# Four small re-orderings in a four-layer graph network: split pairs of layer 2 from its second chunk on, one exponential ahead of a row sum, row tiles ahead of their sets, one piece read a beat sooner

## The reference

```python
# layer 1: attention with 4 heads over all nodes, masked by adj
scores = einsum(q, k) * SCALE + graph_bias * adj
attn   = softmax(where(adj == 0, -1e9, scores));  out = (attn @ v) @ Wout + bout
# layer 2: graph attention
Wh = x @ W;  e = leaky_relu((Wh @ a[:256])[:, None] + (Wh @ a[256:])[None, :], 0.2)
h  = softmax(where((adj > 0) | eye, e, -9e15), axis=1) @ Wh
# layers 3 and 4: graph convolution with degrees
d = adj.sum(axis=1) ** -0.5
layer 3: (d[:, None] * adj * d[None, :]) @ x @ W.T + b
layer 4: relu((d[:, None] * adj * d[None, :]) @ x @ W)
```

## Time and profile before

| | before |
|---|---|
| median of 3 runs | 2970.06 us (2968.12 to 2972.88) |
| the profiled execution | 2971.03 us, span 2969.0 us |
| PE busy | 2917.2 us, 98% |
| DVE busy | 2134.3 us, 72% |
| ACT busy | 1901.1 us, 64% |
| POOL busy | 761.4 us, 26% |
| chain that ended last | PE 86%, DVE 6%, DMA 2%, issue 2%, ACT 2%, POOL 1% |
| granted clock of TensorE, mean | 0.996 |

### The profile page before, as it was taken

The page is one execution under the profiler, slowest core; times in us unless marked ns, Lnnn a source line. Parts: engine busy times, 40 slices in busy tenths (PEclk is TensorE's granted clock), DMA queues, the critical chain, the costliest instruction groups (busy, mean ns, idle before and its releaser), DMA issues.

```text
span 2969.0 us, 45931 instructions
## 1 busy us (share of the span) xinstructions
PE 2917.2 (98%) x16828; PEld 2195.2 (74%) x16828; DVE 2134.3 (72%) x3633; ACT 1901.1 (64%) x2755; POOL 761.4 (26%) x458
## 2 busy tenths in 40 slices
PE   8999999999999999999999899999999999999998
PEld 6677777777777777777776565555568888788887
DVE  6777777777777777777766999899745656666564
ACT  4677777777777777777777777777753433533332
POOL 2123321333213331233302455555500101000000
PEclk9999999999999999999999999999999999999999
DMA  6556575565745566456617254554279999989882
GB/s 190 148 158 182 178 210 153 164 185 178 214 140 173 185 186 194 140 180 182 193 57 274 107 185 156 166 174 156 75 179 220 218 206 205 226 214 219 200 205 57
DMA packets 387183, 521.86 MB, mean 176 GB/s; under 512 B 38672, under 2 KB 316432, under 8 KB 370576
## 3 DMA queue, kind: packets, MB, share of 16 engines
q1 hardware_dynamic: 361920, 432.41, 53.0%
q10 hardware_dynamic: 18144, 66.07, 7.1%
q0 software_dynamic: 6896, 20.45, 2.4%
HBM read 430.71 MB, written 88.08 MB: 175 GB/s over the span
## 4 chain that ended last, share of the span: by engine, by line
PE 86%; DVE 6%; DMA 2%; issue 2%; ACT 2%; POOL 1%; SPq 1%; POOLq 0%; DVEq 0%; ACTq 0%
PE at_o L615 15%; PE at_turn L589 11%; PE at_turn L602 10%; PE gl_four L1562 9%; PE gl_quad L1619 7%; PE gl_quad L1620 7%; PE gl_quad L1621 7%; PE at_score L589 5%; PE at_score L602 5%; PE gl_quad L1527 3%; PE at_mixed L624 2%; DVE gl_first_weights L1898 1%; DMA gl_early<-x 1%; DVE gl_first_weights L1851 1%; PE at_mixed L569 1%
## 5 line engine op out<-in xcount | busy, mean ns | idle before, releaser
L726 ACT ACTIVATE at_probs<-at_probs,at_minus_max 128x1024 f32<-128x1024 f32 x512 | 581.6, 1139 | 9.6 <-DVE at_minus_max L880 8.7
L875 DVE CUSTOM_DVE_ANT_0 at_probs<-at_turn,at_bias 128x1024 f32<-128x1024 f32 x336 | 407.9, 1214 | 187.1 <-PE at_turn L589 184.3
L512 POOL TENSOR_SCALAR at_masked<-at_bias 128x512 bf16<-128x512 f32 x180 | 365.4, 2050 | 496.3 <-DMA at_bias<-in_adj 404.2
L735 ACT ACTIVATE at_pT<-at_turn 128x1024 f32<-128x1024 f32 x342 | 346.0, 1024 | 219.7 <-PE at_turn L602 219.7
L615 PE MATMUL at_o<-at_pT,at_values 128*64 128x256 f32 x4096 | 470.3, 382 | 0.0
L1736 ACT ACTIVATE gl_split<-gl_units 128x1024 fp32r<-128x1024 f32 x256 | 262.2, 1057 | 263.5 <-PE gl_quad L1621 263.5
L615 PEld LDWEIGHTS at_o<-at_pT,at_values 128*64 128x64 f32 x4096 | 282.5, 137 | 172.8 <-issue 43.2
L1619 PE MATMUL gl_quad<-gl_split,gl_rows_hi 128*128 128x512 f32 x1024 | 399.7, 390 | 3.8 <-DVE gl_split L1968 3.8
L1620 PE MATMUL gl_quad<-gl_split,gl_rows_hi 128*128 128x512 f32 x1024 | 398.6, 389 | 0.0
L1621 PE MATMUL gl_quad<-gl_split,gl_rows_lo 128*128 128x512 f32 x1024 | 398.4, 389 | 0.0
L589 PE MATMUL at_turn<-at_kT,at_q 128*128 128x512 f32 x1344 | 396.0, 416 | 0.6 <-DVE at_maxima L875 0.6
(11 more groups left out here) (158 smaller groups left out, 4091.1 us busy)
## 6 DMA issues: line engine op xcount, KB each, us to landing
gl_units<-adjT SPq DMA_DIRECT2D x512, 256.0 KB, 8.2
at_bias<-in_adj SPq DMA_DIRECT2D x128, 512.0 KB, 6.1
gl_first_weights<-in_adj SPq DMA_DIRECT2D x32, 2048.0 KB, 9.2
at_values<-v_heads ACTq DMA_DIRECT2D x126, 512.0 KB, 4.1
at_probs<-in_adj SPq DMA_DIRECT2D x208, 256.0 KB, 3.4
adjT<-at_probs SPq DMA_DIRECT2D x832, 64.0 KB, 2.6
gl_early<-x SPq DMA_DIRECT2D x160, 128.0 KB, 2.7
adjT<-gl_early SPq DMA_DIRECT2D x192, 64.0 KB, 1.8
```

Source lines behind the costliest of these rows:

```text
L512: pool.tensor_scalar(masked[:, g % MASKS, :], part, 0.0, MASKED / SCALE, ALU.is_equal, ALU.mult)\
L726: act.activation(part, part, ACT.Exp, bias=minus_max[:, k, t:t + 1], scale=1.0, accum_out=sums[:, k, t, pp:pp + 1]).then_inc(prob_ready, 1)
L735: act.activation(pT[:, j % PT_SLOTS, :], place[:], ACT.Copy).then_inc(pT_ready, 1)
L875: dve.tensor_tensor_reduce(out=ring[:, place_in_ring(u, pp), t, :], in0=place[:], in1=bias[:, t, at], scale=SCALE, scalar=LOWEST, op0=ALU. ...
```

## The change

- `READ_AT`: piece 4 is read by VectorE in beat 14 and no longer in beat 15.
- `LAST_EXP` = 11: in pair 11 of a chunk ScalarE takes the exponential first and the row sum second; in all other pairs the order stays.
- SyncE loads row tiles 13 to 23 ahead of sets 0 and 1, and no longer behind them.
- In the first chunk of layer 2 pairs 10, 12 and 14 are multiplied in float32 like the others. The high and low parts of `wh` are made in the second chunk, the low ones in pairs 3 to 5 (before: 5 to 7 of the first), and behind a new wait for the last product of the first chunk, since they overwrite `wh`. The loads of the third chunk no longer wait for split products of the first.

```diff
-    READ_AT = {7: 0, 9: 1, 11: 2, 13: 3, 15: 4}
+    READ_AT = {7: 0, 9: 1, 11: 2, 13: 3, 14: 4}
...
+    LAST_EXP = PAIRS - QP - 1
...
-                for pair in SPLIT_PAIRS:
+                for pair in SPLIT_PAIRS if c else ():
...
-            for m in range(13):
+            for m in range(24):
                 load_row_tile(1, m)
             load_set(0, 0)
             load_set(0, 1)
-            for m in range(13, 24):
-                load_row_tile(1, m)
             load_set(0, 2)
             load_set(0, 3)
...
-                if pair in SPLIT_PAIRS:
+                if c and pair in SPLIT_PAIRS:
                     i = SPLIT_PAIRS.index(pair)
-                    if c == 0:
+                    if c == 1:
                         pe.wait_ge(wh_lo_ready, i + 1)
-                    pe.wait_ge(pT_lo_ready, len(SPLIT_PAIRS) * c + i + 1)
+                    pe.wait_ge(pT_lo_ready, len(SPLIT_PAIRS) * (c - 1) + i + 1)
...
-                if pair in SPLIT_PAIRS:
+                if c and pair in SPLIT_PAIRS:
                     act.activation(pT_hi[:, g % PT_RING, :], pair_bank[g % 2], ACT.Copy).then_inc(pT_ready, 1)
...
-                    if c == 0 and 2 <= pair < 2 + len(SPLIT_PAIRS):
+                    if c == 1 and 2 <= pair < 2 + len(SPLIT_PAIRS):
                         split_wh_hi(pair - 2)
...
+                    if pair == LAST_EXP:
+                        exponential(ITEMS * c + CT + pair)
                     add_rows(ITEMS * c + LEAD + pair)
-                    if pair < PAIRS - QP:
+                    if pair < LAST_EXP:
                         exponential(ITEMS * c + CT + pair)
...
                 dve.wait_ge(wh_hi_ready, i + 1)
+                dve.wait_ge(multiplied1, PAIRS)
...
-                    if c == 0 and 5 <= pair < 5 + len(SPLIT_PAIRS):
-                        split_wh_lo(pair - 5)
-                    if pair in SPLIT_PAIRS:
+                    if c == 1 and 3 <= pair < 3 + len(SPLIT_PAIRS):
+                        split_wh_lo(pair - 3)
+                    if c and pair in SPLIT_PAIRS:
                         keep_pT_lo(c, pair)
```

## The result

| | before | changed |
|---|---|---|
| median, first session | 2969.09 us (2966.87 to 2972.88, 4 runs) | 2953.11 us (2952.43 to 2954.27, 4 runs) |
| ratio to before | | 0.9944, 95% interval 0.9932 to 0.9955 |
| the profiled execution | 2971.03 us, span 2969.0 | 2952.43 us, span 2950.7 |
| the same comparison in a later session | 2973.58 us (2968.54 to 2977.92, 9 runs) | 2955.98 us (2953.84 to 2956.47, 5 runs) |
| its ratio | | 0.9941, 95% interval 0.9929 to 0.9954 |

What follows compares the result with a forecast made beforehand. TensorE, busy 98% of the span, was taken as the bound. Terms -8.3 + 0.2 - 2.5 - 5.0 - 3.1 = -18.7 us took the profiled 2971.03 to 2952.3, as a median 2951.3 us; range 2945.5 to 2958.

Steps and rivals of the forecast that it cites:

- Part 1, first chunk: Layer 2's first chunk: pairs 10, 12, 14 plain, the 13.86 us step becomes 4.31; -8.3 us, ends -10 and -5.
- 0.5 off at turn 4: ScalarE's copy in pair 3 that holds turn 4 moves from first to second chunk: 0.5 us off, 0.5 on.
- Part 1, what is late next: VectorE's shift for the second chunk comes at 1704.1, ScalarE wants it at about 1706: 2 us early.
- Part 1, second chunk: VectorE's 1.8 us of `wh` differences move into pairs 3 to 5, making pair 10's low part 1.2 us later.
- I take 0.2 ... ends 0 and 1.5: Second chunk: TensorE's stall for pair 10's late low part, zero to 0.5 us, taken as +0.2.
- Part 2: Exponential ahead of the row sum in pair 11: -3.9 us over chunks two to seven, +1.4 new stall, net -2.5.
- The degrees' delay: Seventh chunk's later row sum delays the degrees and ScalarE's copy of pair 1 in the last chunk: +1.4 us.
- Part 3: Last chunk: row tiles 13 to 23 issued before the sets remove waits of ScalarE and TensorE; -5.0 us, ends -5.0 and -2.
- a sign of being wrong: ScalarE waiting for row tile 24 in the last chunk, listed among what would show the forecast wrong.
- the fourth rival: Tile 24 late behind four sets and the store, TensorE waits in pairs 12 to 14; price 5, 2956.3 us; chance 0.11.
- the sixth: Rival, slower than before: tile 24 lands so late (2208) that the sum turns positive; price 22, 2973 us; chance 0.03.
- Part 4: Layer 1's end of projections: piece 4 read in beat 14 removes TensorE's 3.18 us wait; -3.1 us, ends -3.5 and -1.

Runs made afterwards that it cites:

- Part 1 undone: Changed kernel with layer 2's first-chunk split pairs, and the making of the `wh` parts there, put back; 2960.77 us.
- Wh moved: Changed kernel with high parts of `wh` made in ScalarE's first-chunk turns 12, 13, 15, low parts in VectorE's second-chunk pair 1; 2950.44 us, again 2952.36.
- the last experiment: Changed kernel with the parts of `wh` moved and, in the last chunk, row tiles 0 to 23 split one pair later; 2949.89 us, ratio 0.9924.
- run 7: Not a follow-up kernel: the last run of layer 3, a stage inside each execution; 49.85 us before, 51.74 in the changed kernel, 50.09 when that ran again.

## Why the prediction was right, step by step

- **Part 1, first chunk.** Forecast -8.3 and 0.5 off at turn 4; measured -8.77. The step was 13.86 and is 4.31, and its two components were both as read: the wait for the low part, and the slow matmuls behind it, which went with it (clock 0.93 to 1.00). "Part 1 undone" brings 9.1 us back.
- **Part 1, what is late next.** The shift of the second chunk was early, as forecast, and no kernel has a wait of TensorE at its first turns. But it was early by 0.6 us (1699.36 to 1699.96) and not by 2. VectorE wrote it 0.8 us later than counted. ScalarE wanted it 0.5 us sooner, because the working left out that turn 14 moves up with the 0.5 gained at turn 4.
- **Part 1, second chunk: mis-sized.** The 0.5 for turn 4 came as said (4.84). The term "I take 0.2 ... ends 0 and 1.5" measured +1.2. The step that failed is "so the low part comes 1.2 us later": it came 2.2 us later. Against the 1.2 us that the row left to spare this gives the wait of 0.96 us. Of its two numbers the 1.8 us of work is right, and so is the 0.6 that goes into waits for stores (VectorE waited 1.54 us for them before, 1.01 now). What the count left out is two delays, which these rows show:

```profile
1717.86 0.69 DVE L1215 TENSOR_SCALAR gl_first_weights<-gl_first_weights 128x1024 f32<-128x1024 f32 x1 [0.65 <-ACT gl_first_weights L1682]
...
1732.01 2.05 DVE L1899 SCALAR_TENSOR_TENSOR gl_first_weights<-gl_first_dst_row,gl_minus_src,gl_first_weights 128x1024 f32<-128x1024 f32 x1
```

VectorE waits 0.65 us for a row sum of ScalarE that the high parts of `wh` pushed back (I had charged them to TensorE's turn alone). And from there to the low part four instructions of VectorE are 0.8 us longer beside a mask of GpSimd, where before there were three (the last section); the additional one is the logits of 2.05 us, which took 1.28 before. Together 1.8 + 0.65 + 0.8 - 0.6 would be 2.65 us; the 0.45 beyond the measured 2.2 is lost in small shifts on the way. "Wh moved" has three of these again, and no such wait for the row sum. Its gain of 1.7 us is the 0.5 at turn 4 and the 1.2 at pair 10. How it divides between high and low parts was not tried. The 1.2 us is inside the ends but six times the value taken.
- **Part 2.** In "changed" it is 0.70 to 0.72 in chunks 3, 4, 5 and 7, forecast 0.65. In the second it gave nothing, since the late low part holds the same turn. In the sixth it was 0.05 in "changed", 0.18 and 0.45 in two others, and 0.61 to 0.74 in seven, as the low parts there were late or not. The degrees' delay, forecast +1.4, measured +1.29, with the stall at the instruction that was named. Its cause was shown by two kernels that take it away in two ways, the row sum first in the seventh chunk and the tiles one pair later.
- **Part 3.** Forecast -5.0, measured -5.0 (the step 9.31 is 4.31). Tile 24 cost nothing, as forecast, and close to the forecast's own count: the four sets had landed 54.7 us behind the chunk's start, which is 2186.9 on the old scale, where the prediction had 2185 to 2188. ScalarE was 0.3 us from a wait for it, which the prediction names as a sign of being wrong. TensorE was some 5 us from one: the 2.9 us of the prediction are only ScalarE's idle time behind the tile, and the next copy is then still not wanted at once. In the last experiment ScalarE waits 5.02 us and TensorE not at all. So a wait of ScalarE, as it came in later kernels, was not yet the fourth rival; the sixth wanted the tile at 2208 on the old scale, and it came at 2187.1. The prediction left open whether the store of the rows would keep its pace beside four sets or wait for all of them. It kept its pace: its last DMA landed at 2161.3, 9.1 us behind its issue as beside two sets, while the sets landed until 2170.7. So the trace agrees with the rule that the prediction cited of the Trainium skill, "DMA: Bandwidth & Descriptors", "Queues, rings and completion order", that a DMA engine takes turns between queues.
- **Part 4.** Forecast -3.1, measured -3.05, of which 0.9 was the clock of one execution. The gap at 82.5 did not vanish as forecast; a shorter one of 0.85 us ends at 83.13, and one of 0.67 follows. The mechanism is shown; the wait itself is worth 2.2, and up to 3.05 where the clock falls behind it.
- **Layers 3 and 4, and the start.** Forecast 0. The trace had +1.5 and -2.4. The +1.5 is run 7, most of it a fall of the clock in this one execution. The -2.4 is scatter as far as the other traces tell: 1.15 us lies ahead of beat 14, 1.3 in the rest of layer 1. The sum of the stages that the change touches is -17.4 us (-3.05 - 8.77 + 1.01 - 2.91 - 3.72), the forecast's -18.7; of the 1.3 between them 1.0 is the second chunk's and 0.6 the sixth's, and the rest has the other sign. The two comparisons of medians, -16.0 and -17.6, fit it.

## What to carry to other kernels

Where one engine carries 98% of the time, count an edit by that engine's starts, step by step, and ask of every stall removed what stands 1 or 2 us behind it: here a sum with five such steps came within 1.3 us of the stages that the change touches. Count the spare time as carefully as the gain: one margin here was 0.6 us where 2 had been counted, and another some 5 where 2.9 had been. Work moved out of a full stretch should go to where its engine has slack, and every instruction that the engine then issues later must be counted, down to a row sum that a third engine waits for. A part worth less than the scatter of the whole can still be settled, if the stage it acts in repeats from run to run: undo it alone and read that stage.

## What the runs showed of the hardware

One thing was not in the forecast's count at all. VectorE and GpSimd disturb each other in layer 2 in a regular way. In "changed", VectorE and GpSimd at one place:

```profile
1749.66 1.21 DVE L1852 CUSTOM_DVE_ANT_0 gl_first_weights<-gl_first_dst_row,gl_first_weights 128x1024 f32<-128x1024 f32 x1
...
1750.81 2.05 DVE L1899 SCALAR_TENSOR_TENSOR gl_first_weights<-gl_first_dst_row,gl_minus_src,gl_first_weights 128x1024 f32<-128x1024 f32 x1
...
1753.92 1.27 DVE L1899 SCALAR_TENSOR_TENSOR gl_first_weights<-gl_first_dst_row,gl_minus_src,gl_first_weights 128x1024 f32<-128x1024 f32 x1
```

```profile
1749.94 4.43 POOL L1215 TENSOR_SCALAR gl_first_weights<-gl_first_weights 128x1024 f32<-128x1024 f32 x1
```

The same logits take 1.27 us alone and 2.05 beside GpSimd's mask. In this trace GpSimd has 61 such masks, and 45 instructions of VectorE are about 0.8 us longer than their kind; each of the 45 lies beside one mask, and starts 3.5 to 3.7 us before that mask's end (42 of them 3.48 to 3.57). The instructions of VectorE that follow beside the same mask have their usual length, but for some short ones that start in the mask's last 0.7 us and take up to 0.5 us longer. So a mask costs VectorE about 0.8 us once, some 36 us in this layer (45 x 0.8), and it is one of these, the logits at 1732.01, that helped to make the low part of the second chunk late. GpSimd is held up as well. 43 of the 61 masks last over 3.7 us (up to 4.70, the shortest 3.62), and each of the 43 ends 3.5 us after the end of the VectorE instruction that was running when it began: here the maximum of 1749.66 ends at 1750.87 and the mask at 1754.37. The Trainium skill, "SBUF — State Buffer", "Who interferes with whom", says that GpSimd and a VectorE instruction with two SBUF inputs or in a two-port mode exclude each other for the whole instruction of whoever came first; the trace agrees for GpSimd, whose masks run their 3.5 us only once VectorE's instruction is done. It does not agree for VectorE, which is held for 0.8 us and not for the 3.5 us that the mask still lasts.

The second is how close the waits are. A low part that starts 47.8 us behind its chunk's start costs nothing, at 48.5 it costs 0.46 us of waiting, at 49.6 it costs 0.96 beside a turn that is itself 0.5 late. That is how the same code has chunks of 67.99 and of 68.68 us in different executions.
